# K turned by VectorE and a round of transfers through DRAM instead of TensorE transposes, in a graph-attention kernel

## The reference, cut to what matters

```python
z_l, z_g, v = x @ W_lang.T, x @ W_grav.T, x @ W_V.T          # per batch, 512 x 512 each
zn  = z_l / max(norm(z_l), EPS)
A_l = max(zn @ zn.T, 0) * not_eye
A_g = exp(-max(sq + sq.T - 2 * z_g @ z_g.T, 0) / (2 * sigma**2)) * not_eye   # sq: row sums of z_g**2
K_l = A_l * adj / row_sum;  K_g = A_g * adj / row_sum
K   = w_l * K_l + (1 - w_l) * K_g
out = layernorm(x + (K @ v) @ W_O.T)
```

## Time and profile before

| what | before |
| --- | --- |
| median of 3 timed runs | 1020.04 us |
| span of the profiled execution, first to last instruction | 1016.6 us |
| TensorE busy | 1002.1 us (99%) |
| VectorE busy | 646.2 us (64%) |
| ACT busy | 322.4 us (32%) |
| bytes through the DMA queues | 55.04 MB |

### The profile page before, as it was taken

How to read it: one execution, slowest core, us unless ns; L and a number is a source line. 1 busy time by engine, 2 the same in 40 slices (tenths; PEclk the granted TensorE clock), 3 DMA queues, 4 the chain that set the end, 5 groups by cost and what they waited for, 6 DMA issues and landing times.

```text
span 1016.6 us, 15123 instructions
## 1 busy us (share of the span) xinstructions
PE 1002.1 (99%) x5194; PEld 867.0 (85%) x5194; DVE 646.2 (64%) x1786; ACT 322.4 (32%) x632; POOL 151.8 (15%) x155
## 2 busy tenths in 40 slices
PE   9999999999999999999999999999999999999997
PEld 7788888888888888888888889888898888888885
DVE  4565757657485674757757586574856748477488
ACT  4333233232422333233232332324233232242341
POOL 1202111021200212102021100212001121010231
PEclk9999999999999999999999999999999999999999
DMA  8320130403104040140401304031040401403001
GB/s 218 72 43 1 46 80 5 121 0 94 31 21 104 0 117 7 42 84 0 124 0 59 66 11 113 0 97 28 21 103 0 114 11 42 83 0 125 1 21 63
DMA packets 155378, 55.04 MB, mean 54 GB/s; under 512 B 133824, under 2 KB 137920, under 8 KB 155328
## 3 DMA queue, kind: packets, MB, share of 16 engines
q1 hardware_dynamic: 153216, 53.49, 20.9%
q10 hardware_dynamic: 2112, 1.05, 0.4%
HBM read 37.75 MB, written 16.78 MB: 54 GB/s over the span
## 4 chain that ended last, share of the span: by engine, by line
issue 66%; PE 20%; POOL 11%; DVE 2%; POOLq 0%; DMA 0%; ACT 0%; DVEq 0%
POOL mask_r L1014 6%; PE ring L283 5%; PE ring L285 5%; PE ring L284 4%; POOL rstd L1021 3%; PE g_bank L283 2%; PE g_bank L285 2%; PE g_bank L284 2%; POOL r L1008 1%; PE g_bank L278 1%; PE ring L278 1%; POOL u_odd_lo L996 1%; PE g_bank L321 0%; DMA y<-in_x_dram 0%; DVE al L823 0%
## 5 line engine op out<-in xcount | busy, mean ns | idle before, releaser
L660 DVE TENSOR_TENSOR zl_lo<-ring,zl_hi 128x512 fp32r<-128x512 f32 x64 | 44.1, 691 | 117.3 <-ACT zl_hi L525 117.3
L569 ACT ACTIVATE off<-g_bank 128x128 f32<-128x128 f32 (+1 forms) x128 | 40.4, 331 | 227.8 <-DVE diag_out L736 227.3
L1021 POOL TENSOR_TENSOR rstd<-var_eps,neg_half 128x1 f32<-128x1 f32 x64 | 46.0, 719 | 410.2 <-DVE var_eps L855 410.2
L283 PE MATMUL ring<-xT_hi,wgT_hi 128*128 128x512 f32 x256 | 101.6, 397 | 0.0
L283 PE MATMUL ring<-xT_hi,wlT_hi 128*128 128x512 f32 x256 | 101.4, 396 | 0.0
L283 PE MATMUL ring<-wvo_hi,xT_hi 128*128 128x512 f32 x256 | 101.0, 395 | 0.0
L285 PE MATMUL ring<-xT_hi,wlT_lo 128*128 128x512 f32 x256 | 99.9, 390 | 0.0
L285 PE MATMUL ring<-wvo_hi,xT_lo 128*128 128x512 f32 x256 | 99.8, 390 | 0.0
L285 PE MATMUL ring<-xT_hi,wgT_lo 128*128 128x512 f32 x256 | 99.8, 390 | 0.0
L284 PE MATMUL ring<-xT_lo,wgT_hi 128*128 128x512 f32 x256 | 99.8, 390 | 0.0
L284 PE MATMUL ring<-xT_lo,wlT_hi 128*128 128x512 f32 x256 | 99.8, 390 | 0.0
(11 more groups left out here) (121 smaller groups left out, 2248.8 us busy)
## 6 DMA issues: line engine op xcount, KB each, us to landing
xb<-in_x_dram SPq DMA_DIRECT2D x60, 256.0 KB, 4.7
out_dram<-y SPq DMA_DIRECT2D x60, 256.0 KB, 2.0
y<-in_x_dram SPq DMA_DIRECT2D x14, 1024.0 KB, 5.7
y<-in_x_dram SPq DMA_DIRECT2D x4, 256.0 KB, 5.3
al<-in_L_gnn_W_grav_dram ACTq DMA_DIRECT2D x4, 256.0 KB, 5.9
ag<-in_L_gnn_W_lang_dram SPq DMA_DIRECT2D x1, 1024.0 KB, 9.8
xb<-in_L_gnn_W_V_dram SPq DMA_DIRECT2D x1, 1024.0 KB, 11.9
mask_r<-in_L_gnn_W_O_dram SPq DMA_DIRECT2D x4, 256.0 KB, 9.1
```

The lines of the kernel that those rows point to most:

```text
L283: nc.tensor.matmul(psum, lh, rh, start=k == 0, stop=False)
L569: nc.scalar.activation(off[:, mine[0]:mine[-1] + 1, :], g_bank[i][:, j0 * P:(j0 + len(mine)) * P] .rearrange("p (c n) -> p c n", n=P), ACT ...
L660: nc.vector.tensor_tensor(pair[1][:, i, :], bank[:, :], pair[0][:, i, :].bitcast(F32), ALU.subtract).then_inc(evacuated, 1)
L1021: nc.gpsimd.tensor_tensor(rstd[:, i:i + 1], var_eps[:, i:i + 1], neg_half[:, 0:1], ALU.pow)\
```

## The change

K of batches 0 to 13 is no longer transposed by TensorE. VectorE transposes each row tile of `al` in 32x32 squares into `ag`, with the squares of one group of 32 columns side by side. SP stores the row tile (256 KB, 2 KB per partition) to a tensor in DRAM, `k_turned`, and loads it back into `al` in four transfers of 64 KB, each to 32 partitions in pieces of 512 bytes; between the store of tile i and the loads of tile i stands the store of tile i + 1. ACT makes the hi part from `al` in SBUF and VectorE the lo part, each with an access pattern that puts the blocks in order. `kT` leaves the list of tiles of the ring.

VectorE's order changes: the subtraction of zl 2 comes after the first two `mask_al`, that of zl 3 after the first `combine`, the turns of K follow the combinations, and u 1 comes after all of them. SP's list is shifted: x of batch b + 3 is loaded at the head of a step, ahead of the stores of batch b, then the residual of batch b + 1, then K of batch b + 1. SP's loop has 13 rounds of one batch. The last two batches keep TensorE's transposes; in their list the subtraction of zl 3 comes after the scales.

```diff
 BATCH = ([("zg", 1, 0), ("hsq", 0, 0), ("zg", 1, 1), ("zg", 1, 2), ("zg", 1, 3), ("zl", 1, 0), ("r", 0, 0),
-          ("zl", 1, 1), ("zl", 1, 2), ("zl", 1, 3), ("u", 1, 0), ("u", 1, 1), ("u", 1, 2), ("kT", 0, 0),
-          ("u", 1, 3), ("kT", 0, 1), ("out", 0, 0), ("kT", 0, 2), ("out", 0, 1), ("kT", 0, 3), ("out", 0, 2),
-          ("out", 0, 3)])
+          ("zl", 1, 1), ("zl", 1, 2), ("zl", 1, 3), ("u", 1, 0), ("u", 1, 1), ("u", 1, 2), ("u", 1, 3)]
+         + [("out", 0, i) for i in range(4)])
...
+        k_turned = nc.dram_tensor("k_turned", [T, P, N], F32).ap()
+        k_by_part = k_turned.rearrange("t (b j) (d r) -> t d j b r", j=Q, d=QN)
...
-            def batch(b, parity, stream):
-                sp.wait_ge(whole_transposed, b * T + 2 * T)
-                load_blocks(xb, x_blocks[b + 2], xb_loaded)
+            def turn_k(b):
+                for i in range(T):
+                    sp.wait_ge(k_blocks, b * T + (i + 1))
+                    sp.dma_start(k_turned[i], ag[:, i, :]).then_inc(k_stored[i], 16)
+                    if i:
+                        fetch_k(b, i - 1)
+                fetch_k(b, T - 1)
+            def fetch_k(b, i):
+                sp.wait_ge(k_stored[i], b * 16 + 16)
+                for d in range(QN):
+                    sp.dma_start(al[d * Q:(d + 1) * Q, i, :].rearrange("j (b r) -> j b r", b=QN),
+                                 k_by_part[i, d]).then_inc(k_loaded[i], 16)
+            def load_x(b):
+                sp.wait_ge(whole_transposed, b * T)
+                load_blocks(xb, x_blocks[b], xb_loaded)
+            def turns(b, residual=True):
+                if residual:
+                    load_residual(b)
+                turn_k(b)
+            def batch(b):
+                load_x(b + 3)
                 store_rows(b)
-                load_residual(b + 1)
+                turns(b + 1)
...
-            all_batches(sp, batch, last_two)
+            load_x(2)
+            turns(0, residual=False)
+            with sp.Fori(0, B - 3) as step:
+                batch(step)
+            store_rows(B - 3)
+            load_residual(B - 2)
+            last_two(B - 2, None)
...
-                for i in range(3):
+                for i in range(T):
                     s.project("u", i)
-                s.transpose_k(0, 0)
-                s.project("u", 3)
-                s.transpose_k(0, 1)
                 for i in range(T):
-                    s.aggregate(0, i, parity)
-                    if i + 2 < T:
-                        s.transpose_k(0, i + 2)
+                    s.aggregate(0, i, parity, by_dma=True)
...
+                def hi_k(self, i):
+                    act.wait_ge(k_loaded[i], self.b * (16 * QN) + 16 * QN)
+                    nc.scalar.activation(kT[0][:, i, :].rearrange("p (k b i) -> p k b i", k=T, i=Q),
+                                         al[:, i, :].rearrange("p (b k i) -> p k b i", k=T, i=Q), ACT.Copy)\
+                        .then_inc(kT_hi_written, 1)
...
-                s.hi("kT", 0, 0, kT)
+                s.hi_k(0)
                 s.hi("u", 1, 3, u[1 - parity])
-                s.hi("kT", 0, 1, kT)
+                s.hi_k(1)
                 for k in range(T):
                     whole_hi_part(b + 2, k, xT)
                     if k + 2 < T:
-                        s.hi("kT", 0, k + 2, kT)
+                        s.hi_k(k + 2)
...
+                def turn_k(self, i):
+                    dve.wait_ge(k_ready, self.rows(0, i))
+                    nc.vector.transpose(ag[:, i, :].rearrange("p (d k i) -> p k d i", d=QN, i=Q), al[:, i, :])\
+                        .then_inc(k_blocks, 1)
+                def lo_k(self, i):
+                    dve.wait_ge(kT_hi_written, self.rows(0, i))
...
-                s.lo("zl", 1, 2, zl)
                 s.mask_al(0, 0)
                 s.mask_al(0, 1)
-                s.lo("zl", 1, 3, zl)
+                s.lo("zl", 1, 2, zl)
                 s.mask_al(0, 2)
                 s.mask_al(0, 3)
                 s.scale_of_al(0)
...
+                s.combine(0, 0)
+                s.lo("zl", 1, 3, zl)
+                s.turn_k(0)
+                s.combine(0, 1)
                 s.lo("u", 1, 0, u_next)
-                s.combine(0, 0)
-                s.combine(0, 1)
-                s.lo("u", 1, 1, u_next)
+                s.turn_k(1)
                 s.combine(0, 2)
                 s.combine(0, 3)
+                s.turn_k(2)
+                s.turn_k(3)
+                s.lo("u", 1, 1, u_next)
                 s.lo("u", 1, 2, u_next)
-                s.lo("kT", 0, 0, kT)
+                s.lo_k(0)
                 x_transpose(b + 2, 0)
                 s.lo("u", 1, 3, u_next)
-                s.lo("kT", 0, 1, kT)
+                s.lo_k(1)
                 for i in range(T):
                     if i + 1 < T:
                         x_transpose(b + 2, i + 1)
...
                     s.residual(0, i)
                     s.row_sums(0, i)
                     if i + 2 < T:
-                        s.lo("kT", 0, i + 2, kT)
+                        s.lo_k(i + 2)
```

More of the change, by code:

```diff
@@ L204, in graph_attention @@
             sem("bn_written"), sem("moments"), sem("var_ready"), sem("rstd_ready"), sem("y_done"))
+        k_blocks = sem("k_blocks")
+        kT_hi_written = sem("kT_hi_written")
+        kT_split = sem("kT_split")
+        k_turned = nc.dram_tensor("k_turned", [T, P, N], F32).ap()
+        k_by_part = k_turned.rearrange("t (b j) (d r) -> t d j b r", j=Q, d=QN)
+        k_stored = [sem(f"k_stored{i}") for i in range(T)]
+        k_loaded = [sem(f"k_loaded{i}") for i in range(T)]
         block = ctx.enter_context(nc.Block())
@@ L433, in transpose_k, with aggregate @@
                     transposed(bank, [al[:, i, j * P:(j + 1) * P] for j in range(T)]).then_inc(stream_ready, 1)
-                def aggregate(self, db, i, parity):
+                def aggregate(self, db, i, parity, by_dma=False):
                     bank = self.begin(("out", db, i))
-                    pe.wait_ge(evacuated, self.stream.upto(("kT", db, i)))
+                    if by_dma:
+                        pe.wait_ge(kT_split, self.b * T + (i + 1))
+                    else:
+                        pe.wait_ge(evacuated, self.stream.upto(("kT", db, i)))
                     kT_i = [t[:, i, :].rearrange("p (k n) -> p k n", n=P) for t in kT]
@@ L825, in combine @@
                         op0=ALU.mult, op1=ALU.add).then_inc(k_ready, 1)
+                def turn_k(self, i):
[4 more added lines that the diff above has]
+                    dve.wait_ge(kT_hi_written, self.rows(0, i))
+                    nc.vector.tensor_tensor(kT[1][:, i, :].rearrange("p (k b i) -> p k b i", k=T, i=Q),
+                                            al[:, i, :].rearrange("p (b k i) -> p k b i", k=T, i=Q),
+                                            kT[0][:, i, :].bitcast(F32).rearrange("p (k b i) -> p k b i", k=T, i=Q),
+                                            ALU.subtract).then_inc(kT_split, 1)
                 def y(self, db):
```

## The result

The changed kernel takes 1012.97 us (median; 1012.77 to 1014.65), the kernel before 1020.01 in the same session: a ratio of 0.994, 95% interval 0.9928 to 0.9952. It is faster by 7 us; 13.2 were forecast. The profiled span goes from 1016.6 to 1011.3 us, and TensorE is busy 19 us less than before, so most of what was taken off its list came back as waiting.

What follows compares the result with a forecast made beforehand. TensorE's instruction list was taken to bound the kernel. 8 x 1.42 (batches without a jump) + 6 x 0.6 (with one) - 6 x 0.3 (x's move) = 13.2 us, so 1020.0 - 13.2 = 1006.8 us; range 997 to 1022.

Steps and rivals of the forecast that it cites:

- transposes taken off TensorE: Four groups of transposes leave TensorE's list in 14 batches: 1.92 us per batch, 26.9 us, the most that can be gained.
- TensorE's wait before out 3: VectorE's lo part of kT 3 comes after out 3 is due, so TensorE waits 0.5 us per batch.
- extra loss at the jumps: At six jumps back, TensorE's idle time at the mirror grows by 0.8 us; moving x costs 0.3 more each.
- the round trip: K's store to DRAM and load back is covered by u 1's and u 2's products, with 0.1 to 0.6 us slack.
- x ahead of the stores: x's load, moved ahead of the stores, may slow VectorE's code fetch: 0.3 us per jump taken, bounds 0 and 4.7.
- Rival B: At each jump, code loading under the x load takes 1.5 us longer: 1014 us; at full 4.7, 1033; chance 0.15.
- VectorE's list: In the out phase, kT 2's subtraction starts 3.91 us after u 3's, and kT 3's another 3.39 later.
- A: At out 0, K's round trip is longer than its cover; at x's 4.7 us landing, 1031 us; chance 0.14.
- D: In VectorE's turns and lo parts, strided access costs 0.33 us more each, so nothing moves: 1020 us; chance 0.05.
- C: In the out phase VectorE keeps up, so only the transposes count: 1020 - 26.9 = 993 us; chance 0.06.

Runs made afterwards that it cites:

- E7: The kernel before with VectorE's loop written out, so no jump back on VectorE: 1014.54 us, ratio 0.9955.
- E6: The changed kernel with x loaded behind the residual, VectorE's loop written out, and lo parts of kT 2 and 3 earlier: 987.94 us, ratio 0.969.
- E2: The changed kernel with VectorE's loop written out as 14 batches in a row, other engines keeping their loops: 998.37 us, ratio 0.9787.
- E8: The changed kernel with VectorE's loop written out and lo parts of kT 2 and 3 earlier, x still ahead of the stores: 988.16 us, ratio 0.9696.
- E5: The changed kernel with K's stores and loads left out, VectorE's turns kept, out computed from an unturned K: 1012.76 us, ratio 0.9948.
- E1: The changed kernel with x of batch b + 3 loaded behind the residual instead of ahead of the stores: 1005.6 us, ratio 0.986.
- E9: The changed kernel with a batch's stores waiting until VectorE has read the next batch's four Gram diagonals, x still ahead: 1005.87 us, ratio 0.9867.
- E4: The kernel before with only x's load moved ahead of the stores, K still transposed on TensorE: 1023.55 us, ratio 1.0043.
- E3: The changed kernel with VectorE's lo parts of kT 2 and 3 ahead of the previous tile's residual and row sums: 1019.32 us, ratio 0.9999.

## Why the prediction was wrong in size

The direction and the mechanism held; the gain was half. Its terms, each against a pair of runs:

| term | forecast | measured | from |
| --- | --- | --- | --- |
| transposes taken off TensorE | 26.9 | 26.6 | E7 - E6, no jump and no wait for kT_lo in either |
| TensorE's wait before out 3 | 0.5 per batch | 0.73 per batch, 10.2 | E2 - E8 |
| extra loss at the jumps | 6 x (0.8 + 0.3) = 6.7 | 14.6 - 4.4 = 10.2 | changed - E2, against before - E7 |
| the round trip | 0 | 0, to 1.4 us | E5 |

26.6 - 10.2 - 10.2 = 6.2 us, against the 7 measured. The terms are steps of one chain of runs from the kernel before to the changed one, so their sum has to come out near it and does not check the split. The difference is mostly the kernel before itself, whose median was 1020.01, 1019.77 and 1018.93 us in the three sessions; with each run against its own session, the wait before out 3 is 9.4 us and the loss at the jumps 10.0.

**The step that failed** is the last term of the sum, "x ahead of the stores": "I take 0.3 per jump". It measured 1.2 (E1). Without it the forecast would have been 1006.8 - 1.8 = 1005.0, and E1, the changed kernel without that move, takes 1005.6. That it comes so near is in part luck: out 3's wait cost 2 to 3 us more than the 14 x 0.5 of the forecast, and what is left of the jumps in E1 (1005.6 - 998.37, less the 4.4 of before) is 2.8 us where 6 x 0.8 = 4.8 were forecast. Rival B had the mechanism, a code fetch under load, and 1014 us for 1.5 us a jump; it was given 0.15. But it looked at the wrong transfer, and at the wrong stop: its sign, a first diagonal 4 us after the last normalisation, did not come (2.95 to 3.40 us at the six jumps). Against it the prediction had "by then the load is nearly through", which holds for the second stop; and it had itself placed the stores behind the load, until 557, but did not put VectorE's second fetch beside them. E9 shows that the loss goes when these stores go. That 4.7 us was given as the upper end and 0.3 taken was a choice with no row behind it. The reading that the stops of before stood "beside queues that were nearly free" was wrong as well. These are the two stops of the earlier trace rows; the DMA engines are busy for about half of each:

```profile
553.26:556.33 3.07, 3.07 (x26) 2.98 (x25) 0.00 (x1) 0.00 (x0) 0.00 (x0) 1.00 0.47 173
557.04:558.64 1.60, 1.60 (x8) 1.06 (x6) 0.00 (x1) 0.28 (x2) 0.00 (x0) 1.00 0.59 159
```

**Out 3's wait.** VectorE's list was foreseen closely: kT 2's and kT 3's subtractions start 3.40 us apart (3.39 forecast), and kT 3's ends 11.36 us after u 3's start (595.52 here), as forecast. The last hundredths are luck: 598.9 + 3.91 + 3.39 is 606.2 and not the 606.05 of the forecast, and the 3.91 us became 3.73.

```profile
602.80 0.68 DVE L876 TENSOR_TENSOR kT_lo<-al,kT_hi 128x512 fp32r<-128x512 f32 x1
...
606.20 0.68 DVE L876 TENSOR_TENSOR kT_lo<-al,kT_hi 128x512 fp32r<-128x512 f32 x1
```

TensorE's side of it is what was left out. Out 2 starts at 603.68 and out 3 would at 606.40; kT_lo is done at 606.88, and out 3 starts at 607.02. The first matmul after the wait is 0.31 us ahead of the second instead of 0.23. So 0.48 us of lateness, about the 0.5 forecast, costs 0.70, with 0.14 of handover and 0.08 of restart.

```profile
603.68 0.41 PE L319 MATMUL ring<-u_even_hi,kT_hi 128*128 128x512 f32 x1
...
607.02 0.47 PE L319 MATMUL ring<-u_even_hi,kT_hi 128*128 128x512 f32 x1 [0.41 <-DVE kT_lo L876]
607.33 0.40 PE L320 MATMUL ring<-u_even_lo,kT_hi 128*128 128x512 f32 x1
```

**The jump.** From the Gram rows' start to the mirror there were 10.1 to 10.9 us before and 11.8 to 12.3 after. VectorE's last normalisation ends 5.05 us after that start instead of 4.50 (0.55 later; 0.8 was forecast, and the longer wait for out 3 took some of it back), and the stops add the rest.

**Right.** The round trip: loads of 64 KB land in 2.1 us (2.3 taken), an issue on SP takes 0.43, kT_hi 0 starts within the 0.5 to 1.1 us named, and rivals A and D fall (E5; strided turns 694 ns, strided lo parts 680). The estimate from the Trainium skill, "DMA: Bandwidth & Descriptors", section "Anatomy of one DMA", was 2.15 us. That page fits its figures to transfers issued by GpSimd, and these are issued by SP; for loads of this size the estimate agrees all the same, for the stores of 256 KB (2.0 us, where it gives 2.6) it does not. The batch without a jump was forecast "near 60.0 us" and has 60.01. C, that VectorE would keep up, is false for the changed kernel and becomes true in E6, at 988 (its 993, less the 4.4 us that the jump costs the kernel before).

```profile
L876 DVE TENSOR_TENSOR kT_lo<-al,kT_hi 128x512 fp32r<-128x512 f32 x56 | 38.1, 680 | 2.7 <-ACT kT_hi L600 2.7
L870 DVE STREAM_TRANSPOSE ag<-al 128x512 f32<-128x512 f32 x56 | 37.8, 694 | 0.0
```

What stays open: why the same move of x costs 7.4 us in the changed kernel and 3.8 in the kernel before. In the profiled runs TensorE's idle time at the mirrors grows by 6.6 us there and by 3.5 here. The second stop grows alike, from about 1.5 to about 2.3 us; the first is 2.95 to 3.40 us there against 2.83 to 2.88 in E1, and here 2.73 to 2.96 at five of six jumps against 3.08 or 3.09 at five of six before, and no run shows why. The clock adds to it: in the changed kernel's profiled run the round with the one drop is 1.7 us longer than the others, and the mean granted clock of its timed runs is 0.993 to 0.996, against 0.998 to 0.999 in E1 and 0.997 to 0.999 both in E4 and in the kernel before.

## What to carry to other kernels

When work is taken off the bounding engine, look next for the point where another engine sets the pace, and count there: a gain upstream of such a point becomes waiting, and a long enough wait can cost the clock as well (E3), so the same edit cost 6 us before the point was removed and gained 9 to 10 us after (E8). Moving a transfer moves everything queued behind it: ask what else uses the queues at the new time of each, code fetches included. The round trip through DRAM was free because its time, here 6.5 us from the first turn to the hi part, lay under work that was there anyway.

## What the runs showed of the hardware

- A jump back stops VectorE twice, about 3 us and 1.6 us here, with one packet of the instruction queue at each. With x's load and 1 MB of stores in a row ahead of the second packet that stop is 2.3 to 2.4 us (changed kernel); without the stores there it is 1.5 to 1.6 (E9), and straight code has neither stop (E2).
- After 2.5 to 3.7 us of idle time before its mirror transposes TensorE's granted clock fell at five of six jumps (E3), and with it the speed of the transposes; after 1.7 to 2.3 us at one of twelve (changed kernel and E5). Writing out VectorE's loop removed the wait.
